# A graph layer's root product moved behind its eight relations, and its output closed on GpSimd's queue

## The reference, cut to what matters

```python
h = jnp.maximum(_layernorm(x), 0.0)
u = h @ root + bias
for r in range(8):
    mask = (edge_type == r)
    sums = segment_sum(h[src] * mask[:, None], dst)
    mean = sums / max(segment_sum(mask, dst), 1.0)
    u = u + mean @ weight[r]
z = concatenate([u, h]) @ w_gate + b_gate
out = x + tanh(u) * z + h * (1.0 - z)
```

## Time and profile before

| | us |
|---|---|
| time, median of 3 runs | 1410.62 |
| lowest and highest run | 1409.28, 1416.18 |
| span of the profiled execution, first to last instruction | 1407.7 |
| TensorE matmul busy, 6205 instructions | 1291.5 |
| VectorE busy, 1260 instructions | 952.5 |
| GpSimd busy, 837 instructions | 754.8 |
| ScalarE busy, 501 instructions | 409.0 |

### The profile page before, as it was taken

The page is one execution under the profiler, slowest core; times in us unless marked ns, Lnnn a source line. Parts: engine busy times, 40 slices in busy tenths (PEclk is TensorE's granted clock), DMA queues, the critical chain, the costliest instruction groups (busy, mean ns, idle before and its releaser), DMA issues.

```text
span 1407.7 us, 20144 instructions
## 1 busy us (share of the span) xinstructions
PE 1291.5 (92%) x6205; PEld 651.6 (46%) x6205; DVE 952.5 (68%) x1260; ACT 409.0 (29%) x501; POOL 754.8 (54%) x837
## 2 busy tenths in 40 slices
PE   2978899999999999999998999998999989786898
PEld 1434344444444445555554445454445445343565
DVE  6889678366565667775675577646666778765777
ACT  5344123214132422321332043223222323432000
POOL 2423088786878426686687558664756464320000
PEclk9998899999999999999999999999999999998999
DMA  6442125215224348777875887769889977648872
GB/s 220 154 173 101 44 52 156 69 45 171 54 59 122 114 158 277 238 237 247 277 209 161 292 267 246 238 210 305 279 254 303 312 230 240 204 138 248 239 226 90
DMA packets 112355, 269.44 MB, mean 191 GB/s; under 512 B 22558, under 2 KB 23061, under 8 KB 112268
## 3 DMA queue, kind: packets, MB, share of 16 engines
q1 hardware_dynamic: 78284, 185.88, 40.2%
q0 software_dynamic: 33984, 82.40, 20.4%
HBM read 203.66 MB, written 87.30 MB: 207 GB/s over the span
## 4 chain that ended last, share of the span: by engine, by line
PE 61%; DVE 13%; DMA 10%; issue 7%; POOL 4%; ACT 2%; DVEq 1%; SPq 1%; POOLq 1%; ACTq 0%
PE ps L1320 52%; PE ps L1278 8%; DMA early<-y_rows,pair 7%; DVE W L937 2%; DMA early<-u_rows 1%; POOL onehot L641 1%; DVE hT L990 1%; DMA W<-in_L_gnn_weight_dram 1%; POOL early L633 1%; DVE hT L985 1%; PE ps L1313 1%; POOL pair L623 1%; DVE early L1147 1%; DVE early L1069 1%; DVE early L1163 1%
## 5 line engine op out<-in xcount | busy, mean ns | idle before, releaser
L1320 PE MATMUL ps<-W,hT 128*128 128x512 f16 (+2 forms) x4740 | 1076.0, 385 | 13.0 <-DVE W L937 13.0
L1320 PEld LDWEIGHTS ps<-W,hT 128*128 128x128 f16 (+2 forms) x4740 | 479.9, 104 | 537.8 <-issue 43.4
L633 POOL DMA_INDIRECT early<-y_rows,pair x200 | 242.1, 1211 | 194.5 <-PE ps L1281 152.4
L606 POOL DMA_INDIRECT table_rows<-edges,table_i x160 | 240.5, 1503 | 100.6 <-issue 100.6
L1278 PE MATMUL ps<-early,onehot 128*125 x800 | 205.9, 385 | 26.6 <-POOL onehot L641 13.1
L641 POOL TENSOR_SCALAR onehot<-iota_d,pair 128x125 f16<-128x125 f16 x185 | 159.9, 864 | 64.2 <-DMA early<-y_rows,pair 58.2
L766 ACT ACTIVATE yhl<-early 128x512 f16<-128x512 f32 x120 | 75.3, 628 | 355.3 <-DVE early L1069 194.2
L937 DVE SCALAR_TENSOR_TENSOR W<-W,wsc 128x2048 f16<-128x2048 f32 x62 | 146.5, 2364 | 13.8 <-ACT W L716 13.7
L1278 PEld LDWEIGHTS ps<-early,onehot 128*125 x800 | 106.8, 137 | 100.4 <-issue 46.6
L716 ACT ACTIVATE W<-W,wsc 128x2048 f16<-128x2048 f32 x62 | 122.6, 1990 | 50.9 <-DVE wsc L932 20.3
L683 ACT ACTIVATE peek_out<-W 128x1024 bf16<-128x1024 f32 x80 | 84.2, 1052 | 94.7 <-DMA W<-in_L_gnn_weight_dram 72.7
(11 more groups left out here) (184 smaller groups left out, 756.0 us busy)
## 6 DMA issues: line engine op xcount, KB each, us to landing
y_rows<-yhl SPq DMA_DIRECT2D x144, 256.0 KB
W<-in_L_gnn_weight_dram SPq DMA_DIRECT2D x31, 1024.0 KB, 7.4
early<-u_rows SPq DMA_DIRECT2D x52, 448.0 KB
u_rows<-early SPq DMA_DIRECT2D x50, 448.0 KB
W<-in_L_gnn_w_gate_dram SPq DMA_DIRECT2D x8, 1024.0 KB, 8.3
early<-in_x_dram SPq DMA_DIRECT2D x9, 512.0 KB, 4.5
hs_rows<-early SPq DMA_DIRECT2D x9, 512.0 KB, 3.2
u_rows<-yhl SPq DMA_DIRECT2D x18, 256.0 KB
```

Source lines behind the costliest of these rows:

```text
L606: pool.indirect_dma_start(out=table_rows, out_offset=bass.IndirectOffsetOnAxis(ap=at_i[:, c:c + 1], axis=0), in_=packed[0:EP, c:c + 1], in ...
L633: pool.indirect_dma_start(out=G[:, b, :], out_offset=None, in_=y_rows[i], in_offset=bass.IndirectOffsetOnAxis(ap=idx[:, b, :], axis=0), bo ...
L1320: last = nc.tensor.matmul(ps[0:rows, n % 4, :], hT[:, m, v_h, k, n0:n0 + rows], Wh[MAT[w][c]][:, v_w, k, :], start=(first and v_h + v_w == ...
```

## The change

Root's product goes behind the last relation: it now takes units 235 to 269 and is done by the scheme, and relation 2 takes its place among the direct products (units 40 to 59). Root's result goes to a memory tensor of its own, `root_rows`.

The sums have four sweeps, of 3, 2, 2 and 1 relations, in place of five, at units 100 to 163, 164 to 207, 208 to 248 and 249 to 268; the first sweep starts from nothing instead of root's rows, so it loads no u. All sums are placed ahead of gate_h.

u is closed during gate_h: when all groups are added, GpSimd's own queue loads for each row tile the sum from `u_rows` and root's rows (40 DMAs in all), and GpSimd adds the two (10 additions of 125 x 1024). The gather ring's five buffers are now used for the high and low parts of u (two), root's rows (two) and a fourth u buffer. Row scale, split, tanh, store and turn of tile j then stand at units 278, 279, 280, 282 and 283 + 3j; the two halves of a turn use PSUM banks 4 and 5. The gate's bias row gets a buffer of its own, and the loads for row tiles 3 and 4 of gate_u go to other buffers, at units 305 and 306.

```diff
-    SWEEPS = [(0, 3), (3, 5), (5, 6), (6, 7), (7, 8)]
+    SWEEPS = [(0, 3), (3, 5), (5, 7), (7, 8)]
-    GEMMS = ["rel0", "rel1", "root"] + [f"rel{r}" for r in range(2, R)] + ["gate_h", "gate_u"]
+    GEMMS = [f"rel{r}" for r in range(R)] + ["root", "gate_h", "gate_u"]
-        if w < PLAIN or (w == W_GH and p in (1, 5, 6)):
+        if w < PLAIN or (w in (W_ROOT, W_GH) and p in (1, 5, 6)):
-    AGG_AT = ([109 + g * 66 // 30 for g in range(30)] + [175 + g * 46 // 20 for g in range(20)]
-              + [222 + g * 24 // 10 for g in range(10)] + [246 + g * 27 // 10 for g in range(10)]
-              + [273 + g * 3 for g in range(10)])
+    AGG_AT = ([100 + g * 63 // 30 for g in range(30)] + [164 + g * 42 // 20 for g in range(20)]
+              + [208 + g * 40 // 20 for g in range(20)] + [249 + g * 20 // 10 for g in range(10)])
-        SPLIT_U[max([STEP_END[FINAL + j] + 2] + [n + 2 for n in TURN_U])] = j
-        TURN_U[max([STEP_END[FINAL + j] + 4, freed - 1] + [n + 3 for n in TURN_U])] = j
+    NCU = 4
+    SCALE_U = {FIRST[W_GH] + 8 + 3 * j: j for j in range(NJ)}
+    SPLIT_U = {n + 1: SCALE_U[n] for n in SCALE_U}
+    TANH_U = {n + 2: SCALE_U[n] for n in SCALE_U}
+    TURN_U = {n + 5: SCALE_U[n] for n in SCALE_U}
+    CLOSED_U = {n + 4: SCALE_U[n] for n in SCALE_U}
+        brow_gate = early[:, 0:D]
+        uhl = [G[:, b, :] for b in (0, 1)]
+        root_in = [G[:, b, :].bitcast(F32) for b in (2, 3)]
+        cu = [ub[:, (NS * NJ - 3 + b) % 3, :] for b in range(3)] + [G[:, 4, :].bitcast(F32)]
...
                 for k in range(len(STEPS)):
+                    if n == STEP_END[k] + 2:
                         store_u(k)
+                        if NJ <= k + 2 < len(STEPS):
                             load_u(k + 2)
+                if n in CLOSED_U:
+                    store_closed(CLOSED_U[n])
...
+            pool.wait_ge(s["u_added"], NG)
+            for b in range(3):
+                pool.wait_ge(s[f"u_stored{(len(STEPS) - 3 + b) % 3}"], 32 * u_stores(len(STEPS) - 3 + b))
+            for j in range(NCU):
+                load_sum(j)
+            for b in range(4):
+                pool.wait_ge(s[f"y_stored{b}"], 16 * NJ * 2 * (W_ROOT + 1) // 4)
+            for j in range(2):
+                load_root(j)
+            for j in range(NJ):
+                u = cu[j % NCU][0:DT, :]
+                pool.wait_ge(s[f"cu_loaded{j % NCU}"], 32 * (j // NCU + 1))
+                pool.wait_ge(s[f"root_loaded{j % 2}"], 32 * (j // 2 + 1))
+                pool.tensor_tensor(u, u, root_in[j % 2][0:DT, :], ALU.add).then_inc(s["u_rooted"], 1)
+                if j + 2 < NJ:
+                    pool.wait_ge(s["u_rooted"], j + 1)
+                    load_root(j + 2)
+                if j >= 2 and j + 2 < NJ:
+                    pool.wait_ge(s[f"cu_stored{(j - 2) % NCU}"], 32 * ((j - 2) // NCU + 1))
+                    load_sum(j + 2)
...
             def row_scale(j):
-                u = ub[0:DT, (FINAL + j) % 3, :]
-                dve.wait_ge(s["u_added"], SPAN[NS - 1][0] + (j + 1) * (SWEEPS[NS - 1][1] - SWEEPS[NS - 1][0]))
+                u = cu[j % NCU][0:DT, :]
+                dve.wait_ge(s["u_rooted"], j + 1)
...
             def turn_u(j, half):
-                if half == 0:
-                    pe.wait_ge(s["u_lo"], j + 1)
-                    if j:
-                        pe.wait_ge(s["uT_b_out"], j)
-                    turned_a[0] += 1
+                pe.wait_ge(s["u_lo"], j + 1)
+                if j == 0:
+                    pe.wait_ge(s["u_added"], NG)
                 else:
-                    pe.wait_ge(s["uT_a_out"], j + 1)
-                    turned_b[0] += 1
-                pe.wait_ge(s["wscale_ready"], maxes[0])
-                o = ps[:, 7, :].bitcast(F16)
+                    pe.wait_ge(s["uT_b_out" if half else "uT_a_out"], j)
+                o = ps[:, 4 + half, :].bitcast(F16)
```

More of the change, by code:

```diff
@@ L137, in gated_rgcn_preln, with u_loads, u_stores @@
     STEP_END = [REST_AT[SPAN[s][0] + (j + 1) * (SWEEPS[s][1] - SWEEPS[s][0]) - 1] for s, j in STEPS]
[L138 to L143, removed]
-        SPLIT_U[max([STEP_END[FINAL + j] + 2] + [n + 2 for n in TURN_U])] = j
-        TURN_U[max([STEP_END[FINAL + j] + 4, freed - 1] + [n + 3 for n in TURN_U])] = j
-    assert len(U_DONE) == NJ and len(TURN_U) == NJ and len(SPLIT_U) == NJ
-    TANH_U = {n + 1: SPLIT_U[n] for n in SPLIT_U}
+    def u_loads(k):
+        return len([i for i in range(NJ, k + 1) if i % 3 == k % 3])
+    def u_stores(k):
+        return len([i for i in range(k + 1) if i % 3 == k % 3])
+    NCU = 4
[4 more added lines that the diff above has]
+    CLOSED_U = {n + 4: SCALE_U[n] for n in SCALE_U}
+    assert len(SCALE_U) == NJ and STEP_END[-1] + 4 <= min(SCALE_U) and max(TURN_U) + 2 < NU
+    assert all(n + 1 >= phase_end(W_GH, 1 if j < HT else 3) for n, j in TURN_U.items())
+    assert all(n + 3 <= FIRST[W_GU] + 2 * j for n, j in TURN_U.items())
     LEAD = 2
@@ L207, in gated_rgcn_preln @@
             SCALE_AT[w] = FIRST[w - 1] + 26
-    SCALE_AT[W_GU] = next(n for n in range(FIRST[W_GH] + 26, FIRST[W_GU]) if n + 1 not in TURN_U and n + 2 not in TURN_U)
     SOURCE = [0, 1, 0, 2, 0, 3, 1]
@@ L405, in load_u @@
                 sweep, j = STEPS[k]
[L406 to L410, removed]
+                of = k - NJ
+                sp.wait_ge(s[f"u_stored{k % 3}"], 32 * (k // 3))
+                sp.wait_ge(s[f"u_stored{of % 3}"], 32 * (of // 3 + 1))
                 for n0, p0, rows in halves(*DTL[j]):
@@ L415, in store_u, with store_closed @@
                 sweep, j = STEPS[k]
[L416 to L419, removed]
+                sp.wait_ge(s["u_added"], SPAN[sweep][0] + (j + 1) * (SWEEPS[sweep][1] - SWEEPS[sweep][0]))
                 for n0, p0, rows in halves(*DTL[j]):
                     sp.dma_start(u_rows[n0:n0 + rows, :], ub[p0:p0 + rows, k % 3, :]).then_inc(s[f"u_stored{k % 3}"], 16)
+            def store_closed(j):
+                b = j % NCU
+                sp.wait_ge(s["tanh_ready"], j + 1)
+                for n0, p0, rows in halves(*DTL[j]):
+                    sp.dma_start(u_rows[n0:n0 + rows, :], cu[b][p0:p0 + rows, :]).then_inc(s[f"cu_stored{b}"], 16)
             def load_part(j, part):
@@ L479, in _ @@
                 if n == 10:
[L480 to L488, removed]
+                    load_brow(brow, bias)
+                if n == unit(W_ROOT, 2, 0):
+                    sp.wait_ge(s[YDONE], 2 * NJ * W_ROOT + 1)
+                    load_brow(brow_gate, b_gate)
                 if n == FIRST[W_GU]:
@@ L493, in _ @@
                         sp.wait_ge(s[f"y_stored{b}"], 16 * NO // 4)
-                    for j, part in ((0, "zh"), (1, "zh"), (2, "x"), (2, "t"), (2, "zh"), (3, "zh")):
+                    for j, part in ((0, "zh"), (1, "zh"), (2, "x"), (2, "t"), (2, "zh")):
                         load_part(j, part)
@@ L670, in _, with load_sum, load_root @@
                                        ALU.is_equal).then_inc(s["tile_ready"], 1)
+            def load_sum(j):
+                k = len(STEPS) - NJ + j
+                pool.wait_ge(s[f"u_stored{k % 3}"], 32 * u_stores(k))
+                for n0, p0, rows in halves(*DTL[j]):
+                    pool.dma_start(cu[j % NCU][p0:p0 + rows, :], u_rows[n0:n0 + rows, :]).then_inc(s[f"cu_loaded{j % NCU}"], 16)
+            def load_root(j):
+                for n0, p0, rows in halves(*DTL[j]):
+                    pool.dma_start(root_in[j % 2][p0:p0 + rows, :], root_rows[n0:n0 + rows, :]).then_inc(s[f"root_loaded{j % 2}"], 16)
+            pool.wait_ge(s["u_added"], NG)
[18 more added lines that the diff above has]
+                    load_sum(j + 2)
         @block.scalar
@@ L1045, in finish @@
                 o = out_no(n)
-                if w == W_ROOT:
-                    half = out_place(o)[2]
-                    rows = LT[out_place(o)[1]][1]
-                    dve.wait_ge(s["gemm_done"], n + 1)
-                    dve.wait_ge(s["brow_loaded"], 16)
-                    dve.wait_ge(s[f"y_stored{o % 4}"], 16 * (o // 4))
-                    nc.vector.scalar_tensor_tensor(out=yf[0:rows, o % 4, :], in0=part[0:rows], scalar=wscale(w, 1)[0:rows],
-                                                   in1=brow[0:rows, half * HC:(half + 1) * HC], op0=ALU.mult,
-                                                   op1=ALU.add).then_inc(s[YDONE], 1)
-                    return
                 if w < PLAIN:
@@ L1229, in _ @@
                     low_weights(w, c)
[L1230 to L1231 removed]
+                if n in SCALE_U:
+                    row_scale(SCALE_U[n])
                 if n in SPLIT_U:
```

80 lines of the change are left out of this document (38 added, 42 removed).

## The result

The changed kernel takes 1389.84 us (median of 8 runs, 1387.19 to 1392.65), the kernel before 1407.67 us beside it (8 runs, 1397.81 to 1416.18). The ratio is 0.9886, with a 95% interval of 0.9858 to 0.9915: faster by 1.1%, and 1.2 us under the 1391 predicted. Against the kernel before the forecast was 19.2 us less, and 17.8 were measured. The profiled execution has a span of 1387.1 us.

The account below looks back on a forecast made before the run. TensorE, by far the busiest engine, was taken as the bound, its idle time and lower clock as winnable. Sums +43.1, gate_h -61.1, gate_u -1.2 make -19.2 on 1407.7: 1388.5, with 2.9 for the median 1391 us; range 1366 to 1404.

Parts of the forecast that it names:

- The stall that goes: gate_h: TensorE's waits for the low half of u, 28.3 us in eight waits, gone or below 5 us.
- The sums: Units 100 to 269: all 200 tiles there, 620.3 us without loss plus 50 lost, 670.3; the stretch +43.1 us.
- I take these as even: Sum stretch: fewer loads of u against less time for each; TensorE's 10.4 us of waits unchanged, within the 50 lost.
- rival 1: Sum stretch: GpSimd paces the sums at 3.52 us a tile, 704 us; 1425 us in all, slower; chance 0.09.
- My 77 us for the last sweep's 25 tiles: Last sum sweep: 25 tiles in 21 units, 54 + 23 = 77 us, to which 9 us were added.
- gate_h without sums: gate_h: 97.4 us of TensorE work plus 6.5 lost, 103.9 against 165.0, -61.1 us; VectorE's work 102 us.
- Rival 2: gate_h: GpSimd's ten additions of 2.1 us hold VectorE up, +21 us; 1412 us, no change; chance 0.10.
- signs of being wrong: Listed observations against the forecast, among them a row of VectorE instructions two us longer than before.
- The closing in time: gate_h: GpSimd's additions, 2.1 us each, done before their row scales, with 3 us of cover; cost nothing.
- gate_u: Unit 305 to the end: 110.2 us plus 9 lost, 119.2 against 120.4, -1.2; units 309 and 310 wait some 3 us each.

Follow-up runs that it names:

- e5: Changed kernel with relations 5 and 6 summed in two sweeps again (five sweeps in the new order): 1413.69 us, ratio 1.0067 to the kernel before.
- e1: Changed kernel with GpSimd's additions cut to two of the 1024 columns of u, all loads kept: 1380.54 us.
- e0: The changed kernel itself, timed again beside the kernel before and other variants on one chip: 1389.01 us.
- e3: Changed kernel with VectorE adding root's rows at the start of each row scale, GpSimd only issuing the loads: 1390.18 us.
- e2: Changed kernel with GpSimd doubling root's rows in place before each addition: 1396.57 us.
- e4: Changed kernel with root's rows added to u by the DMA that loads them, no engine adding: 1385.99 us, ratio 0.9869 to the kernel before.

## Why the prediction was right, point by point

- *The stall that goes.* Right: the waits for the low half went from 28.3 us to none; gate_h lost 55.7 us, 61.1 predicted.
- *The sums.* 664.9 us against 670.3, a loss of 44.6 over the 620.3 without loss, where I took 50; by sweep 7.0, 10.7, 12.5 and 14.4, where I took 9, 13, 12 and 16. The sizes are right, the cause is so in part. I gave the loss to GpSimd's pace; one-hots were the longest wait by name (15.5 us), but the costliest single place is a late load of u. The weak step is "I take these as even". TensorE's waits for the additions into u were even, 10.4 us before and 10.9 after, but not what the loads cost: early stores are worth 11 us here and nothing in the kernel before, and without the merged sweep the change would have been 24 us worse. In that kernel, e5, the stretch came near rival 1's 704 us (691.4), but TensorE waited there above all for additions into u behind late loads (27.5 us), less for one-hots (16.6). (My 77 us for the last sweep's 25 tiles are 3.1 us a tile, not 3.0; nothing hangs on it.)
- *gate_h without sums.* The loss was 11.9 us (109.3 - 97.4) where I took 6.5. I gave VectorE 102 us of work and it was busy 100.7, but for another reason: its own instructions need 87.1 (e1), since two of ten row scales, two of eight copies and two of nine low weights now fall outside the window, and 13.7 are the additions' hold. With 87.1 the forecast for a kernel without the hold would have been near the 98.2 us of e1.
- *Rival 2* was a real mechanism and the wrong size: VectorE lost 13.9 us and not 21: nine additions met an instruction that they hold, most of these when part of the addition was over, and the first addition held nothing. 8.5 us reached the time (e1 against e0). One of the signs of being wrong came with it, VectorE instructions two us longer than before. The rule of the Trainium skill, page "SBUF — State Buffer", section "Who interferes with whom", that the second of the two engines stands still for the other's whole instruction, agrees with the trace: 3.40 and 2.90 us, ending behind the additions' ends. I had it as a case of its own, with a chance of 0.10; it should have been a term of the sum, part of gate_h's loss. I wrote that no row shows a long addition beside a VectorE instruction and that 0.25 us at most was lost so far; both are wrong. The trace of the kernel before has one beside the very line that I took for the price: line 841, 0.16 us as a rule, took 1.90 and ended 0.02 us behind the addition (and 1.41 at 41.80 us beside another):

```profile
9.34 2.12 POOL L581 TENSOR_TENSOR early<-early 128x1024 f16<-128x1024 f32 x1 [2.57 <-ACT early L731]
...
9.58 1.90 DVE L841 SCALAR_TENSOR_TENSOR sd<-mv,sd 128x1 f32<-128x1 f32 x1
```

- *The closing in time.* Right: the first addition began at 1172.5 us, and VectorE never waited for one. Two prices were off, one each way: an addition takes 2.37 us, not 2.1, and eight loads took GpSimd 4.3 us to issue, not 10. So the cover was more than the 3 us that I counted.
- *gate_u.* 120.8 us against 119.2, the loss 10.6 where I took 9. At unit 309 VectorE behind zh is the cause, as written (3.7 us); the 3.0 us at unit 305 are a wait for ScalarE's copy, which I had not counted.

The terms were off by -5.4, +5.4, +1.6 and the unforeseen -2.9, so that the sum came out 1.4 us above the span. The two largest cancelled, which is luck: the sum is better than its parts.

## What to carry to other kernels

Moving work out of a crowded stretch makes another one denser, and there transfers that were early enough become late: look in the new stretch at which step a load is issued, and what its queue waits for ahead of it. Two parts of a change can each lose alone and gain together, so undo them one at a time before you say which one paid. An engine's time is not free because it is idle: here GpSimd's additions cost the kernel what they would have cost on VectorE (1389.0 against 1390.2 us in e3).

## What the hardware showed that I had not expected

- An addition on GpSimd holds only some of VectorE's instructions. In gate_h of the kernel after the low half went from 1.28 us to 3.40, a two-input closing (line 1105) from 0.69 to 2.90, sums of quadrants (line 988) from 2.28 to 3.77 and even a row's shift of two columns from 0.17 to 0.96, while the one-column steps just ahead of it, beside the same addition, stayed at 0.15. Closings of line 1094, which read PSUM and one SBUF operand, took 739 to 751 ns in the one shape that met additions most, as elsewhere. In e2, where more instructions met an addition, row maxima kept their 1.20 to 1.21 us and copies out of PSUM their 0.67 to 0.69.
- It works the other way too: where the low weights, a sum of quadrants or a two-input closing had begun first, GpSimd's addition took 2.69 to 3.02 us instead of 2.37 (four of ten), and once 4.29 in e2.
- GpSimd's addition of 125 x 1024 in float32 took 2.37 us; with one operand in both inputs and as the output (e2) 1.90.
- An adding transfer (112 or 13 rows of a tile) took 7.5 us from issue to landing as a median (5.5 to 11.3) and 0.89 us of GpSimd to issue (e4); a plain load of these rows in the kernel after took 0.54 to issue.
